# Expert stage of a decoder layer: direct scatter into expert regions and accumulation in memory, in place of gather, scatter and a final add

## The reference, cut to what matters

```
def _L0_ffn_ref(x, gate_kernel, w0_kernel, w1_kernel, wo_kernel):      # x: layer-normed, 2048 rows of 256
    gate_logits = jnp.einsum('bsd,de->bse', x, gate_kernel)            # 8 experts
    top_k_weights, top_k_indices = jax.lax.top_k(gate_logits, 2)
    top_k_weights = jax.nn.softmax(top_k_weights, axis=-1)
    combine = jnp.einsum('bsk,bske->bse', top_k_weights, one_hot(top_k_indices))
    h0 = jnp.einsum('bsd,edm->bsem', x, w0_kernel)                     # 256 -> 512
    h1 = jnp.einsum('bsd,edm->bsem', x, w1_kernel)
    inter = silu(h0) * h1
    return jnp.einsum('bse,bsem,emd->bsd', combine, inter, wo_kernel)  # 512 -> 256
x = x + _L0_ffn_ref(_layernorm(x), ...)
```

## Time and profile before

| what | value |
|---|---|
| median of 3 runs | 1079.47 us (1079.37 to 1079.78) |
| profiled execution, span from first to last instruction | 1076.6 us |
| own time of the profiled execution | not given; the three runs are 2.8 to 3.2 us above its span |
| PE (TensorE matmul) busy in the span | 912.2 us, 85% |
| DVE (VectorE) busy | 571.5 us, 53% |
| ACT (ScalarE) busy | 439.0 us, 41% |
| POOL (GpSimd) busy | 286.3 us, 27% |
| mean granted TensorE clock | 0.939 of full speed |

### The profile page before, as it was taken

The page is one execution under the profiler, slowest core; times in us unless marked ns, Lnnn a source line. Parts: engine busy times, 40 slices in busy tenths (PEclk is TensorE's granted clock), DMA queues, the critical chain, the costliest instruction groups (busy, mean ns, idle before and its releaser), DMA issues. The chain is left out here.

```text
span 1076.6 us, 18048 instructions
## 1 busy us (share of the span) xinstructions
PE 912.2 (85%) x5790; PEld 789.3 (73%) x5791; DVE 571.5 (53%) x1600; ACT 439.0 (41%) x1117; POOL 286.3 (27%) x458
## 2 busy tenths in 40 slices
PE   4899989999899999997887969796661599999990
PEld 3689978998799988997757657583621488888880
DVE  5565555565456655565484746566379333223325
ACT  4355645655465545653442323233070222322220
POOL 0133312322133212332011110102166244444430
PEclk9899999999999999999998989898875799999996
DMA  9000000000000000001251240707193011111117
GB/s 347 15 2 2 1 3 2 1 2 1 3 1 2 1 1 1 2 1 29 90 127 32 58 98 0 156 0 156 47 376 125 29 50 49 49 53 54 49 40 244
DMA packets 47142, 61.73 MB, mean 57 GB/s; under 512 B 3361, under 2 KB 39714, under 8 KB 46562
## 3 DMA queue, kind: packets, MB, share of 16 engines
q1 hardware_dynamic: 41218, 48.51, 15.8%
q0 software_dynamic: 3744, 10.23, 3.0%
q10 hardware_dynamic: 2112, 2.10, 0.6%
HBM read 34.74 MB, written 9.31 MB: 41 GB/s over the span
## 5 line engine op out<-in xcount | busy, mean ns | idle before, releaser
L262 POOL TENSOR_TENSOR prob<-prob,rinv 128x128 f32<-128x128 f32 (+1 forms) x256 | 124.4, 507 | 329.9 <-DVE rinv L316 329.9
L290 ACT ACTIVATE prob<-masked,negmax 128x128 f32<-128x128 f32 (+1 forms) x256 | 114.6, 448 | 174.9 <-DVE negmax L373 174.9
L305 DVE TENSOR_TENSOR pT_lo<-bank_t,pT_hi 128x384 fp32r<-128x384 f32 x128 | 70.7, 552 | 60.7 <-ACT pT_hi L274 60.7
L305 DVE TENSOR_TENSOR qT_lo<-bank_q,qT_hi 128x512 fp32r<-128x512 f32 x64 | 44.2, 691 | 95.2 <-ACT qT_hi L274 95.2
L1499 DVE TENSOR_TENSOR f_xT_lo<-bank_o,f_xT_hi 128x256 fp32r<-128x256 f32 x39 | 16.5, 424 | 128.1 <-ACT f_xT_hi L1346 82.0
L38 PE MATMUL bank_s<-kT_hi,qT_hi 128*128 128x128 f32 (+1 forms) x256 | 78.0, 305 | 5.2 <-issue 3.4
L373 DVE CUSTOM_DVE_ANT_0 masked<-bank_s,causal 128x128 f32<-128x128 f32 (+1 forms) x256 | 79.0, 346 | 0.0
L38 PE MATMUL bank_o<-pT_hi,v_hi 128*128 128x256 f32 (+1 forms) x256 | 75.0, 293 | 0.5 <-DVE pT_lo L305 0.5
L1644 PE MATMUL bank_y<-f_Wo,f_interT 128*128 x312 | 73.9, 380 | 0.8 <-ACT f_interT L1341 0.8
L38 PE MATMUL bank_y<-WprojT_hi,oT_hi 128*128 128x256 f32 x256 | 72.6, 284 | 0.0
L40 PE MATMUL bank_y<-WprojT_hi,oT_lo 128*128 128x256 f32 x256 | 72.4, 283 | 0.0
(11 more groups left out here) (320 smaller groups left out, 2600.1 us busy)
## 6 DMA issues: line engine op xcount, KB each, us to landing
b_VW_hi<-b_VWs_hi SPq DMA_DIRECT2D x32, 256.0 KB, 4.8
b_VW_lo<-b_VWs_lo SPq DMA_DIRECT2D x32, 256.0 KB, 5.0
f_W_lo<-in_L_ffn_w_kernel_dram SPq DMA_DIRECT2D x16, 512.0 KB, 9.8
f_Wo<-in_L_ffn_wo_kernel_dram SPq DMA_DIRECT2D x8, 512.0 KB, 8.8
stage<-n_L_attn_weight_qkv_dram SPq DMA_DIRECT2D x3, 1024.0 KB, 9.0
stage_proj<-_L_attn_weight_proj_dram SPq DMA_DIRECT2D x1, 2048.0 KB, 14.2
stage<-in_L_xattn_Wq_dram SPq DMA_DIRECT2D x1, 2048.0 KB, 12.5
b_wo<-in_L_xattn_Wo_dram SPq DMA_DIRECT2D x1, 2048.0 KB, 10.6
```

Source lines behind the costliest of these rows:

```text
L262: pool.tensor_tensor(prob[:, u % 3, a:b], prob[:, u % 3, a:b], rinv[:, u % 4, i:i + 1].to_broadcast([P, b - a]), ALU.mult)\
L290: act.activation(prob[:, s % 3, a:b], masked[:, s % 2, a:b], ACT.Exp, scale=-1.0, bias=negmax[:, s % 4, i:i + 1], accum_out=rowsum[:, s % ...
L305: dve.tensor_tensor(dst.lo, src, dst.hi.bitcast(F32), ALU.subtract).then_inc(free[n], 1)
```

## The change

Feed-forward no longer gathers. `slots` is a region of memory with 2048 rows for each of 8 experts, each row 256 features, the token's number and its weight (258 words). `acc` holds 2048 rows of the result and 128 rows for nobody. Routing runs by group: after each group's logits VectorE picks its experts and computes rank plus 2048 times expert, and GpSimd sends its rows to their slots at once with 8 indirect DMAs (4 tiles, 2 choices). The packed rows have two buffers, so group g waits for the scatters of group g - 2. Tiles are then plain loads of 128 consecutive rows by SyncE, with four row buffers. The output is weighted on its way out of the accumulator and added in memory by an accumulating indirect DMA, each behind the landing of the one before. At the end two DMAs copy `acc` to the output. `slots` and the last rows of `acc` are filled once with rows of nobody, early in self-attention.

```diff
 # self_attention, SyncE: behind the loads of the inputs, ahead of those for cross-attention
+                sp.wait_ge(cm.nobody_made, 2)
+                rows = cm.slots.shape[0] // P
+                sp.dma_start(cm.slots.rearrange("(n p) r -> p n r", p=P),
+                             cm.nobody[:].unsqueeze(1).to_broadcast([P, rows, HID + 2])).then_inc(cm.cleared, 16)
+                sp.dma_start(cm.acc[cm.NT * P:, :], cm.nobody[:, 0:HID]).then_inc(cm.cleared, 16)
 # feed_forward
+    UNROLL, ROWBUFS = 4, 4
-        DVE_SPLITS = ((0, 3), (12, 13, 14, 15))
-        POOL_SPLITS = [i for i in range(2 * E) if i not in DVE_SPLITS[0] + DVE_SPLITS[1]]
+        POOL_SPLITS = (1, 4, 7, 10)
+        DVE_SPLITS = [i for i in range(2 * E) if i not in POOL_SPLITS]
 # SyncE
-                for i in range(6):
+                for i in range(2 * E):
                     load_w(i)
-                for g in range(NG):
-                    sp.wait_ge(xn_ready, GT * (g + 1))
-                    sp.dma_start(view[:, GT * g:GT * (g + 1), :], xn[:, GT * g:GT * (g + 1), :])
...
+                sp.dma_start(acc[0:TOKENS, :].rearrange("(t p) k -> p t k", p=P), x_all[:]).then_inc(x_kept, 16)
+                sp.wait_ge(gate_full, NG)
                 for e in range(E):
                     sp.dma_start(Wo[:, e, :, :], wo[e].rearrange("(c p) n -> p c n", p=P)).then_inc(wo_loaded, 16)
-                load_results(sp, 0)
...
+                sp.wait_ge(table_ready, 2)
                 for g in range(NG):
+                    sp.wait_ge(scattered[g], 16 * 2 * GT)
+                def load_rows(q, j):
+                    wait_added(sp, q, j, 1 - ROWBUFS)
+                    at = sp.value_load(row_of[0:1, bass.ds(count(q, j), 1)], min_val=0, max_val=EMPTY)
+                    n = j // ROWBUFS + 1
+                    sp.dma_start(rows[:, j % ROWBUFS, :], slots[bass.ds(at, P), :]).then_inc(rows_loaded[j % ROWBUFS], 16)
+                all_tiles(sp, load_rows)
+                sp.wait_ge(y_added, 16 * TILES)
+                sp.dma_start(done[0:half, :].rearrange("(n r) k -> n (r k)", n=P),
+                             kept[0:half, :].rearrange("(n r) k -> n (r k)", n=P)).then_inc(stored, 16)
 # GpSimd
+                def scatter(g):
+                    pool.wait_ge(pos_ready, g + 1)
+                    pool.wait_ge(weights_ready, 2 * (g + 1))
+                    pool.wait_ge(ids_ready, g + 1)
+                    for k in range(2):
+                        if k == 1:
+                            pool.wait_ge(xn_again, g + 1)
+                        for t in range(GT):
+                            pool.indirect_dma_start(slots[:, :], bass.IndirectOffsetOnAxis(pos_i[:, g, k, t:t + 1], 0),
+                                                    packed[:, g % 2, t, k, :], None).then_inc(scattered[g], 16)
+                ids(0)
+                ids(1)
+                power(0)
...
+                power(1)
+                split_lo(pool, POOL_SPLITS[0], w_lo_pool)
+                power(2)
+                scatter(0)
+                power(3)
+                split_lo(pool, POOL_SPLITS[1], w_lo_pool)
+                pool.wait_ge(scattered[0], 16 * 2 * GT)
+                ids(2)
+                scatter(1)
+                split_lo(pool, POOL_SPLITS[2], w_lo_pool)
+                pool.wait_ge(scattered[1], 16 * 2 * GT)
+                ids(3)
+                scatter(2)
+                split_lo(pool, POOL_SPLITS[3], w_lo_pool)
+                scatter(3)
+                pool.wait_ge(x_kept, 16)
+                for j in range(TILES):
+                    pool.wait_ge(y_copied, j + 1)
+                    wait_added(pool, None, j, 0)
+                    pool.indirect_dma_start(acc[:, :],
+                                            bass.IndirectOffsetOnAxis(rows[:, j % ROWBUFS, ID:ID + 1].bitcast(I32), 0),
+                                            y[:, j % 2, :], None, compute_op=ALU.add).then_inc(y_added, 16)
 # ScalarE
+                    if g >= 2:
+                        act.wait_ge(scattered[g - 2], 16 * 2 * GT)
+                    act.activation(packed[:, g % 2, :, 1, 0:HID], packed[:, g % 2, :, 0, 0:HID], ACT.Copy)
+                        .then_inc(xn_again, 1)
...
                 copy_xnT(0)
                 split_hi(0)
+                split_hi(1)
                 copy_xnT(1)
+                exp_gap(0)
+                for i in (2, 3, 4):
+                    split_hi(i)
+                exp_gap(1)
                 copy_xnT(2)
+                for i in (5, 6):
+                    split_hi(i)
+                exp_gap(2)
                 copy_xnT(3)
+                for i in (7, 8, 9):
                     split_hi(i)
+                exp_gap(3)
+                for i in range(10, 2 * E):
+                    split_hi(i)
 # VectorE: normalize(g) for g >= 2 waits for scattered[g - 2]; pick_two(g) is 14 instructions on 128x32, place_rows(g) 7
+                layer_norm_stats(1)
+                normalize(0)
+                layer_norm_stats(2)
+                normalize(1)
+                low(1)
+                pick_two(0)
+                layer_norm_stats(3)
+                place_rows(0)
+                pick_two(1)
+                low(2)
+                place_rows(1)
+                normalize(2)
+                low(2)
+                pick_two(2)
+                place_rows(2)
+                normalize(3)
+                low(2)
+                pick_two(3)
+                place_rows(3)
...
+                low(len(DVE_SPLITS) - 7)
 # VectorE, tiles
-                    wait_dma(dve, y_stored, q, j, -2)
-                    dve.tensor_copy(y[:, j % 2, :], bank[Y_BANK][:, 0:HID]).then_inc(y_copied, 1)
+                    wait_added(dve, q, j, -1)
+                    dve.tensor_scalar(y[:, j % 2, :], bank[Y_BANK][:, 0:HID], rows[:, j % ROWBUFS, WEIGHT:WEIGHT + 1],
+                                      None, ALU.mult).then_inc(y_copied, 1)
```

More of the change, by code:

```diff
@@ L1019, in _, with __init__, one, feed_forward @@
                 passes(pe, run)
-def feed_forward(nc, cm, gate, w0, w1, wo, xn_rows, y_rows, out):
+class Steps:
+    def __init__(self):
+        self.n = 0
+    def one(self):
+        self.n += 1
+        return 1
+def feed_forward(nc, cm, gate, w0, w1, wo, slots, acc, out):
     E, HID, MLP = w0.shape
@@ L1225, in _, with ids, power @@
                 pool.memset(minus_half[:], -0.5).then_inc(consts, 1)
-                for g in range(NG):
+                def ids(g):
+                    pool.iota(packed[:, g % 2, :, :, ID].bitcast(I32), pattern=[[P, GT], [0, 2]], base=g * GT * P,
+                              channel_multiplier=1).then_inc(ids_ready, 1)
+                def power(g):
                     if g == 0:
@@ L1350, in _, with low @@
                 copy_it(None, LAST)
-                load_results(act, 1)
+                act.wait_ge(y_added, 16 * TILES)
+                done, kept = out.rearrange("b s k -> (b s) k"), acc[0:TOKENS, :]
+                half = TOKENS // 2
+                act.dma_start(done[half:, :].rearrange("(n r) k -> n (r k)", n=P),
+                              kept[half:, :].rearrange("(n r) k -> n (r k)", n=P)).then_inc(stored, 16)
             @block.vector
             def _(dve):
+                step = Steps()
+                splits = iter(DVE_SPLITS)
+                def low(n):
+                    for _ in range(n):
+                        split_lo(dve, next(splits), w_lo_dve)
                 def layer_norm_stats(g):
@@ L1489, in _ @@
[L1489 to L1495 removed]
+                    if g >= 2:
+                        dve.wait_ge(scattered[g - 2], 16 * 2 * GT)
@@ new lines, in _ @@
+                dve.wait_ge(routed, step.n)
+                dve.tensor_tensor(tile_sums[:], tiles[:].unsqueeze(1).to_broadcast([P, E, E]), before[:], ALU.mult)\
+                    .then_inc(routed, step.one())
+                dve.wait_ge(routed, step.n)
+                dve.tensor_reduce(start[:], tile_sums[:], AX_X, ALU.add).then_inc(routed, step.one())
+                dve.wait_ge(routed, step.n)
+                dve.tensor_tensor(end[:], start[:], tiles[:], ALU.add).then_inc(routed, step.one())
```

513 lines of the change are left out of this document (195 added, 318 removed).

## The result

The changed kernel takes **1097.58 us** (median of 4 runs, 1096.34 to 1098.59) beside 1079.62 us for the kernel before (1079.37 to 1080.65). The ratio is 1.0167, with a 95% interval of 1.0153 to 1.0182: 18 us slower, where 3.5 were forecast. The direction held, and so did the whole range of 1068 to 1116; the forecast of 1083 and 6 to either side did not.

What follows compares the result with a forecast made beforehand. Routing was taken as bound by VectorE, tiles by TensorE, the end by DMA and final additions. Routing +15.0, tiles 0 and end -11.5 gave +3.5 on 1079.5: 1083.0 us, 6 either side at 45%, range 1068 to 1116.

Steps and rivals of the forecast that it cites:

- split 7: Routing: GpSimd's low part queued ahead of batch 2, needing ScalarE's high part 7; 2.4 us, ending at 829.8.
- The pitch of a DMA: Routing: each indirect DMA holds GpSimd 1.00 us and begins 0.30 after the one before; 1.30 each, 41.6 for 32.
- the data land 2.45 us after the start: Routing: landing time of each scatter, so a batch of eight has landed 11.6 us after it begins.
- nothing: Routing: weight loads, x to `acc` (2 MB) and Wo beside the chain were to cost no time.
- third rival: Routing: VectorE and GpSimd block each other in the scatter batches too, some 8 us more, 1091; chance 12%.
- split 10: Routing: GpSimd's low part before batch 3; 2.4 us at best, 1 us added for VectorE working beside it.
- Condition (b): Tiles: landed addition frees a row buffer for the next load; C + L below 7.4 us keeps the 5.15 us tile.
- C: Tiles: the accumulating DMA from start to landing, taken as 4.0 us; at most 4.7 before tiles lengthen.
- L: Tiles: a row load with the register load ahead of it, taken as 2.7 us.
- otherwise: Tiles: only past the 7.4 us bound do transposes and outputs wait, two tiles then taking C + L + 2.9.
- first rival: Tiles: accumulation sets the pace from C = 4.7, giving tiles above 5.2 us and 1089 to 1120; chance 20%.
- second rival: Routing: scatters follow without the 0.30 us gap, 1.05 us each, 8 us back, 1075; chance 20%.

Runs made afterwards that it cites:

- latekeep: Changed kernel with the 2 MB store of x into `acc` issued behind the loads of Wo instead of ahead of them: 1093.48 us.
- hold: Changed kernel with VectorE's last five low parts kept back until the last batch of scatters has landed: 1096.06 us.
- best2: Changed kernel with `nobody` widened, four packed buffers, six row buffers, low parts mostly on VectorE, fewer expert-number register loads, earlier positions for groups 2 and 3: 1074.04 us.
- best3: best2 with four of VectorE's last twelve low parts held back until six DMAs of batch 3 have landed: 1072.56 us.
- plain: Changed kernel with the output scatter of each tile writing instead of accumulating, all waits kept: 1090.40 us.
- shift: Kernel before the change with one unused tensor of 258 words a partition allocated ahead of cross-attention's: 1082.22 us.
- pad: Changed kernel with the tensor `nobody` allocated 320 words a partition wide instead of 258: 1093.06 us.

## Why the prediction was right in its sign and wrong in its size

**Routing, +15.0 forecast, +20.5 measured.** Its chain was the right one link by link: GpSimd's queue, two packed buffers, normalize(3) behind batch 1, ScalarE's high part 7, split 7, batches 2 and 3. Counted from the block's start, and with the 3.7 us by which that is later, forecast and trace are:

| event | forecast | measured | lag |
|---|---|---|---|
| batch 0 starts | 799.2 | 798.4 | -0.8 |
| batch 1 starts | 813.5 | 814.7 | +1.2 |
| batch 1 landed | 825.1 | 827.6 | +2.5 |
| batch 2 starts | 833.8 | 836.3 | +2.5 |
| batch 3 starts | 847.7 | 849.4 | +1.7 |
| batch 3 landed | 859.3 | 864.0 | +4.7 |
| first hidden product | 863.5 | 869.0 | +5.5 |

The pitch of a DMA (1.30 forecast, 1.27 measured) is not in the lags. The first term that failed is "the data land 2.45 us after the start". It is 5.9 for batch 0, on DMA engines that weight loads and then the 2 MB store keep full, and costs 2.0 us on the chain from its start to that of batch 1: 16.3 against a forecast of 14.3, and 14.3 in latekeep. The prediction had put the weight loads and x to `acc` under "nothing", since it asked whether they themselves would be in time and not what they delay. The other is that every DMA keeps its pitch of 1.30. One long DMA and a later landing in batch 1 gave 1.3 us, four in batch 3 gave 3.0. That was the third rival, with its price of 8 and a chance of 12%; hold, best2 and best3 show its mechanism, at up to 1.0 us for a DMA with a low part beside it. One term erred the other way: split 10 was given 1 us for VectorE beside it and took 2.35, as it does alone, which is most of why the lag falls to 1.7. The last 0.8 are SyncE's waits and register work ahead of the first load, for which nothing was set.

**Tiles, 0 forecast, +5.0 measured.** Condition (b) was the right place, and its terms were nearly right: C came out at 3.76 where 4.0 was taken, and L as a rule at 2.9 where 2.7 was taken (0.84 us between the landing and the start of the load, 2.0 to 2.2 for the load). In 34 of the 35 loops C + L is 6.5 to 6.8, below the bound of 7.4, and the 0.7 us of slack are there. In one, the loop shown above, the load took 2.92 while the next accumulation ran, C + L is 7.6, and the tile lost 1.5 us. The step that failed, with the other 3.5 us, is the word "otherwise": it let a row cost nothing as long as the bound is kept. Rows with 0.6 to 1.0 us to spare still cost up to 0.4 us a tile, rows with 2 us to spare (plain) almost none; the reading above, by the expert number's read, is argued. So the first rival's outcome came (tiles above 5.2) by another door than its own: the accumulation's longer landing cost time through the row buffers, not by one accumulation behind the other, and its point of decision, C at 4.7, was never reached.

**End, -11.5 forecast, -10.5 measured.** In the forecast's times the last accumulation starts 1.45 us after the last copy begins; it started 2.05 after, and landed after 3.7. The copy took 9.1 for 8.5, from the 6.0 and 2.5 of the earlier trace rows.

**Cross-attention, nothing forecast, +3.5 measured.** The step that failed is one that was not there: the prediction took unchanged code to be unchanged in time. shift and pad show that a new tensor ahead of others is a part of a change.

**What held.** The fill of `slots` (17 MB, 75.5 us) cost nothing, nor did Wo; GpSimd waited 8.0 us for ScalarE's part 7, where the forecast's times give 7.2; the second rival (DMAs that follow without the 0.30) is out, since the 0.30 stands ahead of nearly every one of the 32.

The Trainium skill (DMA: Bandwidth & Descriptors, Anatomy of one DMA) puts most of a DMA's fixed 2 us down to the receipt of its last write. The prediction inferred from it that an accumulating DMA pays this once, with C near 3. The trace is between the two: adding costs 1.35 us over the plain scatter in plain's run, which is less than a second landing of 2.45, but C is 3.76.

The four misses add up: 3.5 + 5.5 + 5.0 + 1.0 = 15.0, and 3.5 + 15.0 = 18.5, where the spans differ by 18.6.

## What to carry to other kernels

When large transfers are themselves in good time, ask which small transfer is waited for while they run: here a landing came 2.5 to 3.2 us later whenever the DMA engines were full at its start, of loads or of the store, so what counts is when the large ones end. Two engines' conflict over on-chip memory counts for GpSimd's indirect DMAs too, so keep VectorE's work with two on-chip inputs away from a row of indirect DMAs that sets the end. And a buffer ring through memory can cost time before its bound is reached: here 0.6 to 1.0 us of slack was not enough and 2 us was. Round a new tensor's size up (here to 1280 bytes), so that the ones behind it keep their alignment.

## What the runs showed of the hardware that was not expected

- An unused tensor of 1032 bytes a partition ahead of the others lengthened the waits for on-chip to on-chip copies of cross-attention from 24.6 to 28.9 us in four places, and the whole kernel by 2.9 us. 1280 bytes did not.
- GpSimd's indirect DMA of 128 rows holds it 0.96 us, up to 1.99 beside VectorE's two-input instruction on 128 x 1024, and 1.56 when it accumulates. The accumulating one lands 3.76 us after its start, the plain one 2.41.
- On full DMA engines a 128-row scatter landed after 5.2 and 5.9 us beside the 2 MB store, and after 5.2 (latekeep) and 5.8 us (best3, medians) beside loads of 512 KB each; on free ones after 2.7.
- An instruction of VectorE on 39 elements took 2.82 us while GpSimd's split ran, and 0.18 in hold, where the split began later.
- Two copies of 1 MB each from memory to memory, on two queues, took 8.0 and 9.1 us together.
